# First norm and the projection to queries, keys and values merged into one chunked stage

## The chip, the cores and the metric

The kernel runs on one core of a Trainium2 chip. A core has a matrix engine (TensorE, in the profile PE, with its weight loads as PEld), VectorE (DVE), ScalarE (ACT), GpSimd (POOL), and SyncE, whose queue (SPq) issues transfers. The engines run their own programs in order and meet at semaphores. The metric is the time of one execution in microseconds (us); less is better.

## What is computed

Four steps, each added to its input: an attention with rotary positions and keys and values from a latent of 64, a mixture of experts, a selective state-space layer, and a second mixture of experts. Each has a layer norm ahead of it. The change touches the beginning of the first:

```python
x = L0_attn_x                                   # (4, 1024, 128), float32
xn = (x - m) / sqrt(v + eps)                    # layer norm over the last axis
q = (xn @ wq).reshape(B, T, H, D)               # H = 16, D = 8
lat = xn @ w_down                               # 64 wide
k = (lat @ wk_up).reshape(B, T, H, D)
v = (lat @ wv_up).reshape(B, T, H, D)
q = _apply_rope(q, cos, sin); k = _apply_rope(k, cos, sin)
# scores = q k / sqrt(D), by pages of 32 causal; softmax; attn @ v; @ wo
x = x + attention
```

The rest of the computation is not changed.

## The kernel before

The 4096 tokens lie as 32 tiles of 128 tokens on the partitions (`X`), and as 8 chunks of 512 tokens (`CH`), two to a batch. A stage is a block: every engine runs its part and all meet at a barrier behind it.

The first stage is `norm_transpose` with `load_x=True`. SyncE's queue issues X in four transfers, the two identity matrices, and the eight weights and tables of the projection (line 122). VectorE takes the statistics of all 32 tiles (`tile_stats`, line 85), then forms mean and variance for all 32 at once in seven small operations (lines 147 to 153). GpSimd raises to the power -1/2, four columns at a time (line 132, eight times). VectorE normalises a chunk in four operations (line 162), PE turns it in four transposes through the identity (line 175) into one of two PSUM banks, and ScalarE copies it to `xnT` (line 189). Only then comes the barrier.

The second stage is `project_qkv`. For each chunk PE runs w_down (the latent), wq, wq_swap, and from the stored latent wk, wk_swap and the values (lines 299 to 308). The swapped products are those of the neighbouring column, for the rotation. VectorE rotates: `by_cos`, `by_sin` and their sum `rot` (lines 321, 323, 327; called cos, sin and rotation here). The result is split into three bfloat16 parts: ScalarE stores the first (line 367), GpSimd forms the remainder `rest` (line 351), ScalarE stores the second (line 372), and VectorE, one chunk later, the third (line 334). SyncE's queue writes the parts to DRAM (`write_parts`, six transfers a chunk, line 246), waiting for each part. From chunk 2 on it also issues five row loads a chunk (`load_rows`, line 483), which bring the parts back in the attention's layout: 25 in this stage, the remaining ones in the next. ScalarE waits, before it overwrites a half of `parts`, for the writes two chunks back.

PE's code in this stage is a loop; what holds a matmul is `swap_taken` (VectorE has read the previous chunk's swapped products), `lat_stored` and `v_stored` (ScalarE's copies). The third stage is the attention (`attend`), whose PE program starts when the barrier is passed, the rows of group 0 are loaded and the mask rows are in.

Of the kernel before, what the change touches and what calls it, by code (L numbers as in the profile page):

```python
# [11 lines left out]
ALU = mybir.AluOpType  # L12
# [79 lines left out]
def norm_transpose(nc, g, visit, loads=(), load_x=False):  # L92
# [3 lines left out]
    with ExitStack() as ctx:  # L96
# [10 lines left out]
        if load_x:  # L107
            half_set, stats_ready = sem("half_set"), sem("stats_ready")
        x_loaded = g.second_ring_in
        block = ctx.enter_context(nc.Block())  # L110

        @block.sync
        def _(sp):
            if load_x:
                x_tiles = g.x_dram.rearrange("b (n p) e -> p (b n) e", p=P)
                for b in range(B):
                    sp.dma_start(X[:, b * NT // B:(b + 1) * NT // B, :], x_tiles[:, b * NT // B:(b + 1) * NT // B, :]).then_inc(x_loaded[b], 16)
                for dst, name in ((g.ident, "ident"), (g.identb, "identb")):
                    sp.dma_start(dst[:, :], g.w[name]).then_inc(g.consts_loaded, 16)
            for group in loads:  # L120
                for dst, src in group.pairs:
                    sp.dma_start(dst, src).then_inc(group.loaded, 16)

        @block.gpsimd
        def _(pool):
            if load_x:
                pool.memset(half[:, :], -0.5).then_inc(half_set, 1)
                pool.wait_ge(half_set, 1)
# [6 lines left out]
        def _(dve):  # L135
            dve.sem_inc(transposed, TURNS)
            if load_x:
                for b in range(B):
                    dve.wait_ge(x_loaded[b], 16)
                    for n in range(b * NT // B, (b + 1) * NT // B):  # L140
                        last = tile_stats(dve, g, n)
                last.then_inc(stats_ready, 1)
                dve.wait_ge(stats_ready, 1)
# [106 lines left out]
def project_qkv(nc, g, q):  # L250

    with ExitStack() as ctx:
        sb = lambda name, shape, dt=F32: ctx.enter_context(nc.sbuf_tensor(f"qkv_{name}", shape, dt))
        sem = lambda name: ctx.enter_context(nc.semaphore(f"qkv_{name}"))
        xnT, PS = g.xnT, g.PS
        w_down, wq, wq_swap, wk, wk_swap, wv, cos, sin = q.w_down, q.wq, q.wq_swap, q.wk, q.wk_swap, q.wv, q.cos, q.sin
        latT = sb("latT", [LAT, 2, CH])
        by_cos, by_sin, rest = (sb(n, [P, 2, CH]) for n in ("by_cos", "by_sin", "rest"))
        rot = sb("rot", [P, 2, 2, CH])
        parts, part_ready, written = g.parts, g.part_ready, g.written  # L260
# [3 lines left out]
        block = ctx.enter_context(nc.Block())  # L264

        @block.sync
        def _(sp):
            for k in range(2):
# [9 lines left out]
            for b in range(B):  # L278
                for k in range(CPB):
                    if CPB * b + k < NCH - 1:  # L280
                        write_parts(sp, g, b, k)
                    if CPB * b + k == CPB:
                        for half in range(CPB):
                            sp.wait_ge(written[half], 2 * WRITES)
# [6 lines left out]
        def _(pe):  # L291
            pe.wait_ge(q.loaded, q.all)
# [2073 lines left out]
```

## Time and profile before

| | us |
|---|---|
| median of 3 runs | 1381.78 |
| lowest, highest | 1377.9, 1382.5 |
| profiled execution, its own time | 1377.09 |
| its span | 1375.2 |
| norm stage, until the first projection matmul | 28.8 |
| projection, PE's first to last matmul | 28.8 to 76.3 |
| first matmul of the attention | 87.96 |
| PE busy over the span | 1223.8 (89%) |

The profile is one execution, recorded per instruction. A line of time gives the start and the length of an instruction or of a run of like ones, and in brackets how long its engine was idle before and whose work ended that. Starts are what to compare; a matmul's end is modelled.
### The profile page before, as it was taken

Reading aid. Unit: us, or ns where it says so; the run is one execution under the profiler, and the core shown is the slowest. Engines: PE = TensorE matmul, PEld = TensorE weight load, DVE = VectorE, ACT = ScalarE, POOL = GpSimd, SP = SyncE. Lnnn points to the kernel's source line nnn. Section 1 sums busy time; section 2 is a strip of 40 time slices with the busy share of each in tenths; the row PEclk is TensorE's granted clock in tenths of the full one; section 3 lists DMA queues with packets and bytes.
Section 4 is the critical chain, followed back from the end, with each engine's and each line's share of the span. In section 5 each row is a group of like instructions: output and inputs, shape, how many; then the busy total and the mean of one; then the engine's idle time right before and its main releaser. Section 6 shows DMA issues by size and latency. Waiting matters only on the chain. (4 is left out here: it accounts for less than half of the span.)

```text
span 1375.2 us, 23176 instructions
## 1 busy us (share of the span) xinstructions
PE 1223.8 (89%) x8438; PEld 641.1 (47%) x8438; DVE 1090.1 (79%) x1339; ACT 849.8 (62%) x1505; POOL 573.9 (42%) x424
## 2 busy tenths in 40 slices
PE   4948999999899979899996966999999999975998
PEld 2412343334343435454443334655565556564665
DVE  5779899999899556856554866999999999974554
ACT  2525899899799633232222778989999899602221
POOL 2330000000101138666675024888888889820000
PEclk9966999999999999999996986999999999995999
DMA  4331111321211175333451001322232223111321
GB/s 112 107 125 43 53 54 55 107 64 49 73 48 51 42 104 165 95 104 102 117 97 22 0 6 48 106 91 95 93 98 101 92 92 105 65 29 28 60 61 39
DMA packets 70527, 103.17 MB, mean 75 GB/s; under 512 B 12599, under 2 KB 42247, under 8 KB 70423
## 3 DMA queue, kind: packets, MB, share of 16 engines
q1 hardware_dynamic: 69126, 100.47, 25.7%
q10 hardware_dynamic: 1296, 1.33, 0.3%
q8 instruction: 64, 1.05, 0.3%
q14 instruction: 41, 0.33, 0.1%
HBM read 88.00 MB, written 13.37 MB: 74 GB/s over the span
## 5 line engine op out<-in xcount | busy, mean ns | idle before, releaser
L626 DVE TENSOR_REDUCE att_found<-PS 128x2 f32<-128x1024 f32 (+2 forms) x288 | 332.8, 1219 | 17.7 <-PE PS L735 16.1
L702 ACT ACTIVATE att_prob<-PS 128x512 f32<-128x512 f32 x576 | 313.5, 596 | 44.6 <-PE PS L757 32.8
L1923 POOL TENSOR_TENSOR ms_ch<-xnT,ms_c_rows 128x1024 f32<-128x1024 f32 x103 | 243.8, 2368 | 45.5 <-PE PS L1833 33.4
L1833 PE MATMUL PS<-ms_ch,ident_sb 128*128 128x512 f32 x512 | 241.2, 593 | 1.0 <-POOL ms_ch L1923 1.0
L1884 DVE TENSOR_TENSOR_SCAN xnT<-xnT,PS 128x1024 f32<-128x1024 f32 x103 | 231.1, 2268 | 7.4 <-PE PS L1824 7.1
L1862 ACT ACTIVATE ms_scaled<-m_dtu_turns,m_bt 128x256 f32<-128x256 f32 x448 | 191.6, 495 | 29.5 <-PE PS L1824 29.5
L776 PE MATMUL PS<-att_prob,att_v 128*32 128x256 f32 (+1 forms) x2560 | 184.2, 374 | 2.8 <-ACT fr_out L691 2.6
L1824 PEld LDWEIGHTS PS<-ident_sb,ms_scaled 128*128 128x128 f32 x1024 | 120.6, 144 | 80.1 <-DVE xnT L1884 37.4
L1824 PE MATMUL PS<-ident_sb,ms_scaled 128*128 128x128 f32 x1024 | 137.0, 278 | 9.7 <-ACT ms_scaled L1862 4.6
L735 PE MATMUL PS<-kr,qr 55*128 55x128 bf16 (+4 forms) x1152 | 120.8, 291 | 25.1 <-DVE att_found L626 13.4
L1250 ACT ACTIVATE f_h<-PS,e_w_b 128x512 f32<-128x512 f32 x64 | 43.9, 687 | 137.6 <-PE PS L1401 129.1
L757 PE MATMUL PS<-qr,kr 55*128 55x128 bf16 (+4 forms) x1152 | 115.2, 278 | 13.6 <-ACT att_prob L702 7.5
L1833 PEld LDWEIGHTS PS<-ms_ch,ident_sb 128*128 128x128 f32 x512 | 87.4, 191 | 64.6 <-issue 61.2
L1869 ACT ACTIVATE xnT<-m_dt,m_a 128x1024 f32<-128x1024 f32 x103 | 116.9, 1136 | 0.0
L735 PEld LDWEIGHTS PS<-kr,qr 48*128 48x128 bf16 (+1 forms) x1152 | 39.5, 97 | 133.4 <-issue 94.9
L1231 POOL TENSOR_TENSOR f_yT<-f_yT,f_prod 128x512 f32<-128x512 f32 x56 | 71.1, 1270 | 68.7 <-DVE f_prod L1343 67.5
L1333 DVE SCALAR_TENSOR_TENSOR f_x3s<-PS,e_w_b,f_mask_row 128x512 f32<-128x512 f32 x64 | 48.0, 750 | 61.2 <-PE PS L1405 60.5
L1219 POOL TENSOR_TENSOR f_xm<-xnT,f_gate_row 128x512 f32<-128x512 f32 x64 | 81.3, 1271 | 13.0 <-DMA f_gate_row<-gate_rows_dram 10.7
L776 PEld LDWEIGHTS PS<-att_prob,att_v 128*32 128x32 f32 x2560 | 55.1, 109 | 62.7 <-issue 53.8
L1410 PE MATMUL PS<-f_h,e_w_w 128*128 128x512 f32 x128 | 66.7, 603 | 6.8 <-DVE f_prod L1343 6.7
L2239 ACT ACTIVATE f_sg<-PS 128x512 f32<-128x512 f32 x40 | 23.9, 597 | 78.5 <-PE PS L2222 78.5
L585 POOL TENSOR_TENSOR att_neg<-att_zero,att_row_max 128x32 f32<-128x32 f32 x16 | 4.1, 254 | 162.7 <-DVE att_row_max L639 162.7
(237 smaller groups left out, 1776.6 us busy)
## 6 DMA issues: line engine op xcount, KB each, us to landing
ms_c_rows<-bc_rows_dram SPq DMA_DIRECT2D x64, 512.0 KB, 3.7
f_gate_row<-gate_rows_dram SPq DMA_DIRECT2D x64, 256.0 KB, 3.6
f_mask_row<-mask_rows_dram SPq DMA_DIRECT2D x64, 128.0 KB, 3.2
qk_parts_dram<-parts SPq DMA_DIRECT2D x48, 128.0 KB, 1.9
heads_dram<-fr_out SPq DMA_DIRECT2D x16, 256.0 KB, 2.7
f_mask_row<-mask_rows_dram SPq DMA_DIRECT2D x64, 64.0 KB, 3.3
qr<-qk_parts_dram SPq DMA_DIRECT2D x32, 96.0 KB
qr<-qk_parts_dram SPq DMA_DIRECT2D x96, 32.0 KB
```

The costliest lines, as they stand in the source:

```text
L626: dve.tensor_reduce(found[:, :, pair, first:first + (n - 1) * step + 1:step], PS[:, bank:bank + 2, :].rearrange("p r (w n) -> p r w n", w= ...
L702: act.activation(prob[:, step % PROB_RING * GH + h, :], PS[:, SCORE_BANK + unit % SCORE_RING, :], ACT.Exp, scale=float(D) ** -0.5).then_in ...
L735: last = pe.matmul(PS[:, MAX_BANK + 2 * (m % 2) + r, at:at + n], rows(qr, count, i, pair, r, q_block * P, P), rows(kr, count, i, pair, r, ...
L757: last[r] = pe.matmul(PS[:, SCORE_BANK + (unit + r) % SCORE_RING, col:col + w], rows(kr, count, i, pair, r, j * P, P), rows(qr, count, i, ...
L776: last = pe.matmul(PS[VW * h:VW * (h + 1), VALUE_BANK, q - half * CH:q - half * CH + w], v1[:, i % 2, half, h, j, :], prob[:, step % PROB_ ...
L1219: pool.tensor_tensor(xm[:, e % XM_RING, :], xnT[:, c * CH:(c + 1) * CH], gate_row[:, e % ROW_RING, :], ALU.mult).then_inc(xm_ready, 1)
L1824: last = pe.transpose(PS[:, X_BANK + 2 * half + k // TPC, k % TPC * P:(k % TPC + 1) * P], scaled[:, s % 2, k, half, :], g.ident[:, :])
L1833: last = pe.matmul(PS[:, Y_BANK + 2 * half + q, :], g.ident[:, :], ch[:, half, q * CH:(q + 1) * CH], start=n == 0, stop=n == NS - 1)
L1862: last = act.activation(scaled[:, s % 2, i, :, :], m.dtu_turns[:, TB * b + i, :, :], ACT.Identity, scale=m.bt[:, at:at + 1])
L1869: act.activation(decay_then_h(s, half), m.dt[:, half, sequence(b)], ACT.Exp, scale=m.a[:, half, n:n + 1]).then_inc(decay_ready, 1)
L1884: dve.tensor_tensor_scan(decay_then_h(s, half), decay_then_h(s, half), inputs(half), 0.0, ALU.mult, ALU.add).then_inc(scanned, 1)
L1923: pool.tensor_tensor(ch[:, half, :], decay_then_h(s, half), c_rows[:, s % C_RING, :], ALU.mult).then_inc(ch_ready, 1)
```

## The change

`norm_transpose` no longer serves the first norm; its work moves into `project_qkv`, one block for both. Without the first barrier:

- The eight weights and tables are issued by ScalarE's queue at the start (line 439 of the new file); SyncE's queue issues X, the identities and then the page masks.
- Mean and variance are formed for one batch (8 tiles) at a time: `moments(b)`. `root(b)` on GpSimd takes 8 columns at once. `tmp`, `mean` and `rstd` are small double buffers.
- VectorE normalises chunks 0 and 1, finishes all statistics, and then, in the loop, rotates chunk c, makes the third part of c-1 and normalises c+2; after chunks 1 and 3 it forms the moments of batches 2 and 3.
- PE turns chunks 0 and 1, projects 0, and then for each c turns c+1 and projects c. The turned chunk goes into the latent's bank 6 (chunk 1 into the values' bank 7), so wq comes first and w_down waits for ScalarE's copy of the turned chunk.
- ScalarE copies chunk c+1 (`store`), then the latent of c, then splits c-1.
- All loops are written out instead of running with a register.

The second norm stage is the same code, now counted as the first visit.

```diff
-                norm_transpose(nc, g, 0, [weights], load_x=True)
                 attention(nc, g, weights, f)
...
-                norm_transpose(nc, g, 1, [m, m.last])
+                norm_transpose(nc, g, 0, [m, m.last])
...
         @block.tensor
         def _(pe):
-            pe.wait_ge(q.loaded, q.all)
+            def turn(c):
+                pe.wait_ge(normed, c + 1)
+                if c >= 2:
+                    pe.wait_ge(lat_stored, c - 1)
+                for j in range(TPC):
+                    last = pe.transpose(PS[:, turn_bank(c), j * P:(j + 1) * P], xn[:, c % 2, j, :], ident[:, :])
+                last.then_inc(turned, 1)
+
+            def project(c):
+                k, x = c % 2, xnT[:, c * CH:(c + 1) * CH]
+                pe.wait_ge(x_stored, c + 1)
+                pe.matmul(PS[:, 2 * k, :], wq[:, :], x, start=True, stop=True)
+                if c + 1 < NCH:
+                    pe.wait_ge(x_stored, c + 2)
+                pe.matmul(PS[0:LAT, LAT_BANK, :], w_down[:, :], x, start=True, stop=True).then_inc(lat_done, 1)
+                pe.wait_ge(swap_taken, c + 1)
+                pe.matmul(PS[:, SWAP_BANK, :], wq_swap[:, :], x, start=True, stop=True)
+                pe.wait_ge(lat_stored, c + 1)
+                pe.matmul(PS[:, 2 * k + 1, :], wk[:, :], latT[:, k, :], start=True, stop=True).then_inc(qk_done, 1)
...
+            turn(0)
+            turn(1)
+            pe.wait_ge(q.loaded, q.all)
+            project(0)
+            for c in range(1, NCH):
+                if c + 1 < NCH:
+                    turn(c + 1)
+                project(c)
...
         @block.vector
         def _(dve):
...
+            def normalize(c):
+                b = c // CPB
+                dve.wait_ge(rstd_ready, b + 1)
+                if c >= 2:
+                    dve.wait_ge(turned, c - 1)
...
+            statistics(0)
+            moments(0)
+            statistics(1)
+            normalize(0)
+            normalize(1)
+            moments(1)
+            statistics(2)
+            statistics(3)
+            dve.wait_ge(q.loaded, q.all)
+            for c in range(NCH):
+                rotate(c)
+                if c >= 1:
+                    third(c - 1)
+                if c + 2 < NCH:
+                    normalize(c + 2)
+                if c in (1, 3):
+                    moments(c // 2 + 2)
+            third(NCH - 1)
...
         @block.scalar
         def _(act):
...
+            for dst, src in q.pairs:
+                act.dma_start(dst, src).then_inc(q.loaded, 16)
+            act.preload_act_table(ACT.Copy)
+            store(0)
+            store(1)
+            latent(0)
+            for c in range(1, NCH):
+                if c + 1 < NCH:
+                    store(c + 1)
+                latent(c)
+                split(c - 1)
+            split(NCH - 1)
```

PE, from the program's start on the loop of the projection, before. `norm_xn` and `qkv_xn` are normalised tiles, `qkv_latT` the stored latent; in brackets stand the semaphores that a row waits for.

```order
L302 MATMUL PS<-xnT,qkv_w_wq_swap 128x512 [waits qkv_swap_taken]
L304 MATMUL PS<-qkv_latT,qkv_w_wk 128x512 [waits qkv_lat_stored]
L305 MATMUL PS<-qkv_latT,qkv_w_wk_swap 128x512
L308 MATMUL PS<-qkv_w_wv,qkv_latT 128x128 [waits qkv_v_stored]
L308 MATMUL PS<-qkv_w_wv,qkv_latT 128x128 x3
L299 ISA
L299 MATMUL PS<-xnT,qkv_w_w_down 64x512
L300 MATMUL PS<-xnT,qkv_w_wq 128x512
```

The same engine and place now, from the projection of chunk 0 into that of chunk 1:

```order
L304 MATMUL PS<-xnT,qkv_w_wq_swap 128x512 [waits qkv_swap_taken]
L306 MATMUL PS<-qkv_latT,qkv_w_wk 128x512 [waits qkv_lat_stored]
L307 MATMUL PS<-qkv_latT,qkv_w_wk_swap 128x512
L310 MATMUL PS<-qkv_w_wv,qkv_latT 128x128 [waits qkv_v_stored]
L310 MATMUL PS<-qkv_w_wv,qkv_latT 128x128 x3
L293 MATMUL PS<-ident_sb,qkv_xn 128x128 [waits qkv_lat_stored,qkv_normed]
L293 MATMUL PS<-ident_sb,qkv_xn 128x128 x3
L299 MATMUL PS<-xnT,qkv_w_wq 128x512 [waits qkv_x_stored]
L302 MATMUL PS<-xnT,qkv_w_w_down 64x512 [waits qkv_x_stored]
```

Between the values of a chunk and the first matmul of the next now stand four transposes, and the first of them waits for `qkv_normed`.

VectorE in the projection's loop, before: the rotation of chunk 1, the third part of chunk 0 and the start of chunk 2.

```order
L321 TENSOR_TENSOR qkv_by_cos<-PS,qkv_w_cos 128x1024 [waits qkv_rotated,qkv_qk_done]
L323 TENSOR_TENSOR qkv_by_sin<-PS,qkv_w_sin 128x1024 [waits qkv_swap_done]
L325 REGISTER_ALU [waits qkv_cos_taken]
L327 TENSOR_TENSOR qkv_rot<-qkv_by_cos,qkv_by_sin 128x1024 [waits qkv_rest_ready,qkv_swap_taken]
L333 REGISTER_ALU
L334 TENSOR_TENSOR parts<-qkv_rest,parts 128x1024 [waits part_ready1]
L321 TENSOR_TENSOR qkv_by_cos<-PS,qkv_w_cos 128x1024 [waits qkv_rotated,qkv_qk_done]
```

The same place now:

```order
L363 TENSOR_TENSOR qkv_by_cos<-PS,qkv_w_cos 128x1024 [waits qkv_rotated,qkv_qk_done]
L365 TENSOR_TENSOR qkv_by_sin<-PS,qkv_w_sin 128x1024 [waits qkv_swap_done]
L369 TENSOR_TENSOR qkv_rot<-qkv_by_cos,qkv_by_sin 128x1024 [waits qkv_rest_ready,qkv_swap_taken,qkv_cos_taken]
L374 TENSOR_TENSOR parts<-qkv_rest,parts 128x1024 [waits part_ready1]
L354 TENSOR_SCALAR qkv_xn<-X,qkv_mean,qkv_rstd 128x128 [waits qkv_turned,qkv_rstd_ready]
L354 TENSOR_SCALAR qkv_xn<-X,qkv_mean,qkv_rstd 128x128 x3
```

The normalising of chunk 3 now stands behind the rotation of chunk 1 and the third part of chunk 0.

## Rows read from the trace of the kernel before

**Rows 1.** Stage table: stretch, its length, busy us of each engine, PE clock, DMA share, GB/s.

```profile
core 0: us, PE busy (x) PEld busy (x) DVE busy (x) ACT busy (x) POOL busy (x), PEclk, DMA share, GB/s
28.80:76.30 47.50, 47.48 (x144) 21.08 (x144) 33.61 (x29) 22.92 (x30) 14.89 (x7) 1.00 0.36 110
87.90:124.40 36.50, 22.96 (x151) 6.52 (x151) 34.70 (x33) 7.67 (x14) 7.24 (x14) 0.50 0.17 51
```

**Rows 2.** Lines of time, program start: start us, length us, engine, line, operation [idle before].

```profile
4.63 1.74 SPq L119 DMA_DIRECT2D ident_sb<-ident  x1
...
4.74 1.65 DVE L85 BATCH_NORM_STATS2 stats<-X 128x6 f32<-128x128 f32 x8 [4.74 <-DMA X<-x]
...
13.23 0.18 DVE L153 TENSOR_SCALAR norm_tmp<-norm_tmp 128x32 f32<-128x32 f32 x1
...
16.08 1.11 PE L175 MATMUL PS<-ident_sb,norm_xn 128*128 128x128 f32 x4 [16.08 <-DVE norm_xn L162]
...
17.33 0.60 ACT L189 ACTIVATE xnT<-PS 128x512 f32 x1 [15.31 <-PE PS L175]
```

**Rows 3.** Transfers issued before 12 us (KB, us to landing), and a stage table row.

```profile
ident_sb<-ident SPq DMA_DIRECT2D x1, 64.0 KB, 5.5
...
5.00:10.00 5.00, 0.00 (x0) 0.00 (x0) 4.67 (x24) 0.00 (x0) 0.00 (x0) 1.00 1.21 287
```

**Rows 4.** Lines of time, first projected chunk.

```profile
28.80 1.96 PE L299 MATMUL PS<-xnT,qkv_w_w_down 128*64 x2 [1.80 <-PEq L96]
...
34.61 1.23 DVE L321 TENSOR_TENSOR qkv_by_cos<-PS,qkv_w_cos 128x1024 f32<-128x1024 f32 x1 [8.78 <-PE PS L304]
```

**Rows 5.** Lines of time, PE and VectorE on chunk 2, and eight normalising operations.

```profile
41.91 1.07 PE L299 MATMUL PS<-xnT,qkv_w_w_down 128*64 x2
...
44.82 1.12 PE L304 MATMUL PS<-qkv_latT,qkv_w_wk 64*128 64x512 f32 x2
...
47.62 0.64 PE L299 MATMUL PS<-xnT,qkv_w_w_down 128*64 x1
...
45.98 1.23 DVE L321 TENSOR_TENSOR qkv_by_cos<-PS,qkv_w_cos 128x1024 f32<-128x1024 f32 x1 [0.97 <-PE PS L304]
...
49.51 1.22 DVE L334 TENSOR_TENSOR parts<-qkv_rest,parts 128x1024 bf16<-128x1024 f32 x1
...
18.03 2.34 DVE L162 TENSOR_SCALAR norm_xn<-X,norm_mean,norm_rstd 128x128 f32 x8 [0.47 <-POOL norm_rstd L132]
```

**Rows 6.** Group of the 128x8 root late in the kernel, and four transposes there.

```profile
L2009 POOL TENSOR_TENSOR mo_rstd<-mo_tmp,half 128x8 f32<-128x8 f32 x4 | 6.6, 1640 | 26.7 <-DVE mo_tmp L2034 26.7
...
1227.20 0.60 PE L1971 MATMUL PS<-ident_sb,mo_xn 128*128 128x128 f32 x4
```

**Rows 7.** Lines of time, end of the projection and start of the attention.

```profile
74.57 1.23 DVE L321 TENSOR_TENSOR qkv_by_cos<-PS,qkv_w_cos 128x1024 f32<-128x1024 f32 x1 [0.97 <-PE PS L304]
...
79.78 1.06 ACT L367 ACTIVATE parts<-qkv_rot 128x1024 bf16<-128x1024 f32 x1 [2.81 <-DMA qk_parts_dram<-parts]
...
84.16 1.23 DVE L334 TENSOR_TENSOR parts<-qkv_rest,parts 128x1024 bf16<-128x1024 f32 x1 [4.78 <-ACT parts L372]
...
87.96 1.04 PE L735 MATMUL PS<-kr,qr 48*128 48x384 bf16 x8 [11.68 <-PEq L252]
...
74.22 2.88 SPq L246 DMA_DIRECT2D qk_parts_dram<-parts  x6
...
80.63 2.86 SPq L246 DMA_DIRECT2D qk_parts_dram<-parts  x6
...
83.54 4.88 SPq L483 DMA_DIRECT2D qr<-qk_parts_dram  x6
```

**Rows 8.** Stage table around two short idle spells of PE, columns as in rows 1.

```profile
139.30:141.50 2.20, 0.16 (x6) 0.11 (x4) 1.27 (x2) 0.22 (x1) 0.00 (x0) 1.00 0.12 14
141.50:144.90 3.40, 3.40 (x36) 1.12 (x34) 1.23 (x1) 2.16 (x4) 0.00 (x0) 0.50 0.26 80
...
779.60:781.90 2.30, 0.27 (x1) 0.00 (x1) 2.30 (x5) 2.30 (x7) 0.00 (x0) 1.00 0.00 0
783.20:786.60 3.40, 3.40 (x5) 1.33 (x4) 3.40 (x7) 2.93 (x5) 0.00 (x0) 0.50 0.00 0
```

More of the change, by code:

```diff
@@ L282, in _ @@
                     if CPB * b + k == CPB:
-                        for half in range(CPB):
-                            sp.wait_ge(written[half], 2 * WRITES)
+                        for part in range(CPB):
+                            sp.wait_ge(written[part], 2 * WRITES)
                     for n in range(begun, min(ROWS_BEGUN, begun + ROWS_A_CHUNK) if b > 0 else 0):
@@ L291, in _ @@
         def _(pe):
-            pe.wait_ge(q.loaded, q.all)
+            def turn(c):
[16 more added lines that the diff above has]
+                pe.matmul(PS[:, 2 * k + 1, :], wk[:, :], latT[:, k, :], start=True, stop=True).then_inc(qk_done, 1)
+                pe.matmul(PS[:, SWAP_BANK + 1, :], wk_swap[:, :], latT[:, k, :], start=True, stop=True).then_inc(swap_done, 1)
+                pe.wait_ge(v_stored, c + 1)
+                for j in range(TPC):
+                    last = pe.matmul(PS[:, V_BANK, j * P:(j + 1) * P], latT[:, k, j * P:(j + 1) * P], wv[:, :], start=True, stop=True)
+                last.then_inc(v_done, 1)
@@ L311, in _, with statistics @@
+            turn(1)
[5 more added lines that the diff above has]
+                project(c)
         @block.vector
         def _(dve):
-            dve.sem_inc(rotated, 1)
-            dve.sem_inc(rest_ready, 2)
-            dve.wait_ge(q.loaded, q.all)
-            def rotate(c, k, before):
+            def statistics(b):
+                dve.wait_ge(x_loaded[b], 16)
+                for n in range(b * TB, (b + 1) * TB):
+                    last = tile_stats(dve, g, n)
+                last.then_inc(stats_done, 1)
@@ new lines, in normalize @@
+            def normalize(c):
[3 more added lines that the diff above has]
+                    dve.wait_ge(turned, c - 1)
+                for j in range(TPC):
+                    n = c % CPB * TPC + j
+                    last = dve.tensor_scalar(xn[:, c % 2, j, :], X[:, c * TPC + j, :], mean[:, b % 2, n:n + 1], rstd[:, b % 2, n:n + 1],
+                                             ALU.subtract, ALU.mult)
+                last.then_inc(normed, 1)
@@ L353, in _, with store @@
+            root(0)
+            root(1)
+            for c in range(NCH):
+                if c in (1, 3):
+                    root(c // 2 + 2)
+                pool.wait_ge(part_ready[0], c + 1)
+                pool.wait_ge(part_ready[2], c + 1)
+                pool.tensor_tensor(rest[:, :, :], rot[:, c % 2, :, :], parts[:, c % 2, 0, :, :], ALU.subtract).then_inc(rest_ready, 1)
         @block.scalar
         def _(act):
-            act.preload_act_table(ACT.Copy)
-            def latent(c, k, reused):
+            def store(c):
+                act.wait_ge(turned, c + 1)
+                act.activation(xnT[:, c * CH:(c + 1) * CH], PS[:, turn_bank(c), :], ACT.Copy).then_inc(x_stored, 1)
```

120 lines of the change are left out of this document (50 added, 70 removed).

## The prediction

> **What bounds the kernel now.** I read the stages first, then the lines of time inside the two that the change merges, then what ends them. The stage table [rows 1] gives the projection 47.5 us, from 28.8 to 76.3, in which PE (TensorE) is busy 47.48: PE is the bound there. The norm ahead of it takes the first 28.8 us: all 32 tiles' statistics must be in before the first moment is formed, and the first projection matmul starts when the last chunk is turned [rows 2, 4]. After 76.3 PE is idle for 11.6 us, until the attention's first matmul at 87.96 [rows 7]. What holds it is the tail of this stage: SyncE's queue issues the row loads of chunk 6 from 83.54, five of which belong to this stage (the sixth row load is already the next stage's), to about 87.6, and VectorE ends its last third part at 85.4 [rows 7]. So 87.6 is the time to beat: everything behind it (1287 us) runs the same code from there, and I let it only shift.
>
> In the steady state before, a chunk costs 5.72 us: the rotation's first product, cos, starts at 45.98 for chunk 2 and at 74.57 for chunk 7, 28.59 over five chunks [rows 5, 7]. PE issues its six matmuls of 0.95 us back to back (41.91 to 47.62) and never waits for VectorE, whose four operations a chunk (4.75 us from the start of cos to the end of the third part, 45.98 to 50.73) run beside the next chunk's matmuls [rows 5].
>
> **Part 1, the start.** The first chunk now needs the statistics of 8 tiles, not of 32, and no barrier. On VectorE: X's first quarter lands at 4.74 before, its statistics take 1.65 [rows 2], seven small operations of about 0.2 each, as the last one's 0.18, 1.5, the root on 8 columns 1.64 (the same operation elsewhere in the kernel [rows 6]), and four normalising operations 1.2 (eight took 2.34 [rows 5]). That is 10.8 if nothing else moved. But the transposes need the identity, which stands behind all of X on SyncE's queue and landed at 4.63 + 5.5 = 10.1 [rows 2, 3]. Now 1.3 MB of weights go at the same time on ScalarE's queue. The transfers moved 287 GB/s while busy [rows 3], and all of it together is 3.5 MB (X 2.1, weights 1.3, identities 0.1), 12.2 us. So the identity lands between 10.1 and 13.9; I take 13.5, near the upper end, because the rate shown was already full with X alone. Issue time is saved on SyncE, but nothing waited for it; the eight issues on ScalarE end long before its first copy.
>
> The Trainium skill ("DMA: Bandwidth & Descriptors", Issuing engines are not separate DMA queues) says the same of the queues: all issuers' transfers run on the same 16 engines, so a second queue saves only sequencer time. If the second queue did add rate, the start would be 2.7 us earlier than I take it, and the total with it.
>
> From the first transpose: four transposes at the low rate and the handover 1.25, the copy 0.60, a handover 0.1 [rows 2], so the first projection matmul starts at 15.4. Before, it took 5.81 from the first matmul (28.80) to cos (34.61), the first alone 1.96 [rows 4]; I keep that, since PE comes equally cold. **cos of chunk 0 starts at 21.2 instead of 34.61: 13.4 us gained.** The statistics and moments of the other batches lie on VectorE before that and fit.
>
> **Part 2, the loop.** Here a wait is added. PE's order is: turn chunk c+1, then project chunk c. The turn waits for `normed`, and VectorE normalises c+1 only after rotating c-1 and making the third part of c-2. "Two chunks ahead" holds for VectorE's normalising; PE turns only one ahead, and as its queue is in order the six matmuls of chunk c, whose input has long been stored, stand behind the turn. VectorE's rotation of c in turn waits for PE's fourth matmul of chunk c. So the two take turns. One round, at PE's full rate:
> - VectorE, from the start of cos: 4.75 to the end of the third part, 1.2 to normalise, 0.1 to hand over: 6.05 [rows 5].
> - PE, from the first transpose: four of them, 0.11 apart, 0.44 (four end after 0.60 [rows 6]). w_down also waits for ScalarE's copy: 0.60 + 0.14 + 0.60 + 0.07 = 1.41, the same as 0.44 + 0.95. Then w_down and wq_swap, 1.91, and 1.16 from the start of wk (44.82) to cos (45.98) [rows 5]: 4.5.
> Sum 10.5 us a round against 5.72. Only wk_swap and the value matmuls (1.9 us of PE) lie beside VectorE's part. The third part of c-1 waits for its split, which ScalarE now begins only after the latent copy of chunk c. That copy ends 1.3 before cos (w_down starts 3.07 before cos; 1.07 for it, 0.1, and 0.6 for the copy), and from the split's start to the third part it took 79.78 to 84.16, 4.4 [rows 7]: ready 3.1 after the start of cos, taken at 3.53, so it does not wait, by 0.4. The moments after chunks 1 and 3 lie under PE's part.
>
> The chunks: chunk 0 has no third part before it, so cos of chunk 1 comes 3.53 + 1.2 + 0.1 + 4.5 = 9.3 later, at 30.5. Five rounds of 10.5 follow: cos of chunk 6 at 83.0. There is no turn ahead of chunk 7, so it follows after PE's own 5.7: 88.7. The tail: third part of chunk 6 done at 88.7 + 4.75 = 93.5, its two writes 1.0, five row loads at 0.81 (83.54, 4.88 for six [rows 7]) 4.1: **98.6, against 87.6: 11.0 us later** with PE at full rate. SyncE's issue chain, which paced the end before, now follows. ScalarE's wait for the writes of chunk 5 (79.78 before [rows 7]) goes, and the chain behind chunk 7 (rotation 3.7, then the 4.4 above, then 1.23: 9.4 from cos) ends at 98.1, just covered. The same 11.6 us idle of PE becomes about 8 before the attention; the clock was at 0.50 through that stage's first 36.5 us [rows 1] and I expect that again.
>
> **Part 3, the clock.** In each round PE is idle 10.5 - 6.2 = 4.3 us. The trace has two shorter idle spells after full work: 139.3 to 141.5, after which the granted clock was 0.50 for 3.4 us, and 779.6 to 781.9, after which it was 0.50 from 783.2 to 786.6 [rows 8]. 0.50 is 1.2 GHz of 2.4. If each of the six spells brings one such stretch wholly over PE's part, PE does 1.7 us less work in each. The bounds are 0, if it falls and recovers within the idle time or not at all, and about 4.5 a round, if PE stays low through all of its part, as over the attention's start [rows 1]. I take 1.5, because some of a stretch will lie in idle time: 6 x 1.5 = 9.0.
>
> The Trainium skill ("TensorE: Matmul & The Clock Gate", HAM oscillation) describes this: bursts of matmuls with waits between lose the full clock again and again. By that rule part 3 recurs in every round; the two spells above agree.
>
> **Sum.** +11.0 + 9.0 = +20.0 us. The profiled run took 1377.1 (span 1375.2), so 1397.1. That run lies below the three timed ones (median 1381.8, lowest 1377.9); putting the base between, at about 1379, gives 1399.
>
> **Rivals.**
> - *The clock holds* (the idle spells cost nothing): +11, 1390. Against it stand both spells of rows 8; for it, that PE comes back to a dense run of 6.2 us each time. If the identity also lands early it is +8.5, 1387.
> - *The clock stays low through most rounds*: six times 4.5 and about 4 for chunk 7 on top of +11, +42, 1421. Against it: in both spells of rows 8 the clock came back after 3.4 us of work. Half of it would be 1410.
> - *It gets faster: the turn's wait is covered.* If normalising c+1 were done when PE comes to its turn, a chunk would cost PE 0.44 + 5.72 = 6.2, SyncE's 6.4 (74.22 to 80.63 [rows 7]) would pace the end, and the 13.4 us of part 1 would mostly stay: about -11, 1368. The sign turns at a round of 10.5 - 11.0/6 = 8.7 us without any clock loss. VectorE's own 6.05 would have to overlap with PE's 4.5 by 1.8 more, and no operation of either can start sooner in the order shown. An error in a duration of 0.2 us does not reach it.
> - *The same*, within 0.3% (about 4 us, what a measurement of this kernel can tell from no change): a round of 8.5 to 9.2 us, between the two.
>
> **How the numbers follow.** Forecast 0.58; the clock holds 0.22; low through most rounds 0.12; faster 0.04; the same 0.04. The likeliest gives 1399. The range reaches from the clock holding with an early start (1387, less 1 for the base) to half way to the low-clock case (1410, plus 2 for the base): 1386 to 1412. Slower holds the first three, 0.92.
>
> **What would show it.** cos of chunk 0 between 18.5 and 22; distance of later cos starts 10.5 to 13, not 5.7; PE's transposes waiting for the normalising on VectorE about 4 us, six times; the first matmul of the attention at 99 to 110; granted clock 0.50 in part of nearly every round. A distance near 6.2 would refute part 2; a clock of 1.00 throughout, part 3; an identity before 11, part 1. I would be wrong as a whole if the attention behind the stage did not just shift.

## The result and the profile after

The changed kernel takes 1405.27 us (median of 4 runs, 1402.15 to 1406.8), the kernel before 1380.78 beside it (4 runs, 1377.9 to 1382.5). The ratio is 1.0184, 95% interval 1.0170 to 1.0199: slower by 24.5 us, inside the forecast's range of 1386 to 1412 and 6 above its middle. The profiled execution took 1405.07 us, span 1403.3. It lies at its median, while the profiled execution before (1377.09) was the fastest of its kind, so the two profiles lie further apart (28.1 us in span) than the medians.

Lines of time of the changed kernel at its start (start us, length us, engine, line, operation [idle before <- what ended it]), to hold against [rows 2]:

```profile
5.02 2.32 SPq L263 DMA_DIRECT2D ident_sb<-ident  x1
5.10 1.64 DVE L85 BATCH_NORM_STATS2 stats<-X 128x6 f32<-128x128 f32 x8 [5.10 <-DMA X<-x]
7.38 0.43 SPq L263 DMA_DIRECT2D identb_sb<-identb  x1
7.96 1.64 POOL L401 TENSOR_TENSOR qkv_rstd<-qkv_tmp,half 128x8 f32<-128x8 f32 x1 [7.10 <-DVE qkv_tmp L345]
9.64 2.14 DVE L354 TENSOR_SCALAR qkv_xn<-X,qkv_mean,qkv_rstd 128x128 f32<-128x128 f32 x8 [0.15 <-POOL qkv_rstd L401]
15.43 1.94 PE L293 MATMUL PS<-ident_sb,qkv_xn 128*128 128x128 f32 x8 [15.43 <-DMA identb_sb<-identb]
17.30 1.19 PE L299 MATMUL PS<-xnT,qkv_w_wq 128*128 128x512 f32 x1
```

Both chunks are normalised by 11.8, and PE waits until 15.43 for the identities. The first matmul of the projection is at 17.30 (28.80 before [rows 4]), the first cos product at 22.77.

One whole round, from the cos product of chunk 2 to that of chunk 3, and the handover to PE in it:

```profile
46.90 1.22 DVE L363 TENSOR_TENSOR qkv_by_cos<-PS,qkv_w_cos 128x1024 f32<-128x1024 f32 x1 [5.15 <-PE PS L306]
50.49 1.22 DVE L374 TENSOR_TENSOR parts<-qkv_rest,parts 128x1024 bf16<-128x1024 f32 x1
51.62 1.11 DVE L354 TENSOR_SCALAR qkv_xn<-X,qkv_mean,qkv_rstd 128x128 f32<-128x128 f32 x4
52.78 1.12 PE L293 MATMUL PS<-ident_sb,qkv_xn 128*128 128x128 f32 x4 [4.23 <-DVE qkv_xn L354]
53.69 1.92 PE L299 MATMUL PS<-xnT,qkv_w_wq 128*128 128x512 f32 x2
55.54 1.94 PE L302 MATMUL PS<-xnT,qkv_w_w_down 128*64 128x512 f32 x2
57.40 1.13 PE L304 MATMUL PS<-xnT,qkv_w_wq_swap 128*128 128x512 f32 x2
58.46 1.12 PE L306 MATMUL PS<-qkv_latT,qkv_w_wk 64*128 64x512 f32 x2
59.62 1.23 DVE L363 TENSOR_TENSOR qkv_by_cos<-PS,qkv_w_cos 128x1024 f32<-128x1024 f32 x1 [6.89 <-PE PS L306]
```

VectorE works from 46.90 to 52.73 and then waits 6.89 us. PE waits 4.23, turns, projects at half speed (a matmul, recorded as two instructions, takes 1.9 us until 57.4 and then 1.1), and hands back. Only wk_swap and the values run beside VectorE's part; the rest of the two parts is one after the other. The waits of PE between 22 and 104 us (total, times, longest) show how often:

```profile
PE PS L293 <- DVE qkv_xn L354: 24.1, 6, 4.2
```

The stage table (columns as in [rows 1]): the six rounds with a turn, two stretches inside them, and the first part of the attention:

```profile
22.80:98.00 75.20, 51.12 (x133) 21.68 (x132) 34.95 (x61) 20.96 (x29) 14.36 (x8) 0.77 0.19 63
26.80:33.60 6.80, 6.07 (x10) 2.04 (x10) 0.67 (x3) 1.91 (x3) 0.00 (x0) 0.51 0.00 0
40.60:43.70 3.10, 2.83 (x7) 1.33 (x8) 1.05 (x8) 0.60 (x1) 1.64 (x1) 0.51 0.25 85
114.90:152.00 37.10, 23.66 (x155) 6.62 (x155) 34.60 (x33) 7.85 (x14) 7.13 (x14) 0.50 0.16 51
```

Where the first row of [rows 1] had PE busy all the time at 1.00, PE is now busy 51.1 of 75.2 us at a mean of 0.77. The second row spans one stretch at 0.50 and the third lies inside another, which lasts 3.4 us (40.5 to 43.9). Four of the six rounds have a stretch of 6.8 us, the second and the sixth one of 3.4. The attention's start looks as it did, at 0.50 for its first 37 us. The end of the stage:

```profile
103.95 1.23 DVE L363 TENSOR_TENSOR qkv_by_cos<-PS,qkv_w_cos 128x1024 f32<-128x1024 f32 x1 [1.11 <-PE PS L306]
106.78 3.20 SPq L227 DMA_DIRECT2D qk_parts_dram<-parts  x6
110.02 5.32 SPq L550 DMA_DIRECT2D qr<-qk_parts_dram  x6
112.15 1.23 DVE L374 TENSOR_TENSOR parts<-qkv_rest,parts 128x1024 bf16<-128x1024 f32 x1 [3.39 <-ACT parts L436]
114.87 1.04 PE L802 MATMUL PS<-kr,qr 48*128 48x384 bf16 x8 [9.21 <-PEq L233]
```

The attention starts at 114.87 against 87.96 [rows 7], 26.9 us later, and the profiled executions end 28.1 apart in span. What lies between shifts, but for 1.2 us.

### The profile page after: what moved, and what is told of

Same layout as the page of the kernel before. It is cut to its first block and busy times, and to the rows that moved or that the text cites. A ratio compares the mean times of both kernels' runs of the same rounds, so it can differ in the third digit from the quotient of the medians.

```text
span 1403.3 us, 22962 instructions
## 1 busy us (share of the span) xinstructions
PE 1236.9 (88%) x8438; PEld 642.7 (46%) x8438; DVE 1091.1 (78%) x1360; ACT 847.3 (60%) x1504; POOL 572.1 (41%) x420
## 5 line engine op out<-in xcount | busy, mean ns | idle before, releaser
L1900 PE MATMUL PS<-ms_ch,ident_sb 128*128 128x512 f32 x512 | 241.2, 594 | 0.9 <-POOL ms_ch L1990 0.9
L1317 ACT ACTIVATE f_h<-PS,e_w_b 128x512 f32<-128x512 f32 x64 | 43.9, 687 | 138.1 <-PE PS L1468 127.8
L1900 PEld LDWEIGHTS PS<-ms_ch,ident_sb 128*128 128x128 f32 x512 | 87.4, 191 | 64.5 <-issue 61.2
L1286 POOL TENSOR_TENSOR f_xm<-xnT,f_gate_row 128x512 f32<-128x512 f32 x64 | 81.1, 1268 | 14.3 <-DMA f_gate_row<-gate_rows_dram 12.7
```

The lines of the kernel that those rows point to most:

```text
L1286: pool.tensor_tensor(xm[:, e % XM_RING, :], xnT[:, c * CH:(c + 1) * CH], gate_row[:, e % ROW_RING, :], ALU.mult).then_inc(xm_ready, 1)
L1900: last = pe.matmul(PS[:, Y_BANK + 2 * half + q, :], g.ident[:, :], ch[:, half, q * CH:(q + 1) * CH], start=n == 0, stop=n == NS - 1)
```

## Experiments

Each kernel differs from the changed one as its diff shows, and was timed beside the kernel before. "cos 0" and "cos 7" are the starts of these products and "attention" that of its first matmul, in the profiled execution. The medians of the kernel before, as measured beside them, lie between 1378 and 1381, so the ratio is what to compare. A round is the time from one cos product to the next.

| kernel | cos 0 | cos 7 | attention | median us | ratio [95%] |
|---|---|---|---|---|---|
| before | 34.61 | 74.57 | 87.96 | 1380.8 | 1 |
| changed | 22.77 | 103.95 | 114.87 | 1405.3 | 1.0184 [1.0170, 1.0199] |
| fill_idle | 23.16 | 91.68 | 102.59 | 1391.5 | 1.0079 [1.0058, 1.0100] |
| norm_first | 22.84 | 69.38 | 80.14 | 1371.3 | 0.9941 [0.9916, 0.9965] |
| turn_inside | 23.62 | 74.42 | 85.00 | 1374.9 | 0.9976 [0.9954, 0.9998] |
| root_later | 22.70 | 72.60 | 83.13 | 1373.8 | 0.9965 [0.9949, 0.9981] |
| pool_beside_2 | 22.50 | 109.41 | 121.58 | 1413.0 | 1.0247 [1.0218, 1.0277] |
| ident_first | 20.34 | 101.19 | 111.83 | 1404.4 | 1.0170 [1.0136, 1.0205] |
| weights_sync | 23.20 | 104.58 | 115.11 | 1404.2 | 1.0176 [1.0157, 1.0195] |
| root_later_ident_first | 20.47 | 71.78 | 82.37 | 1371.9 | 0.9952 [0.9934, 0.9969] |
| norm_root_ident | 19.92 | 67.49 | 78.48 | 1367.3 | 0.9927 [0.9909, 0.9945] |
| norm_first_ident_first_2 | 19.15 | 65.70 | 76.39 | 1364.6 | 0.9910 [0.9883, 0.9937] |
| moments_early_2 | 20.54 | 64.25 | 75.44 | 1367.5 | 0.9922 [0.9899, 0.9945] |

### Is it the place of the normalising on VectorE? (norm_first)

```diff
             for c in range(NCH):
+                if c + 2 < NCH:
+                    normalize(c + 2)
                 rotate(c)
                 if c >= 1:
                     third(c - 1)
-                if c + 2 < NCH:
-                    normalize(c + 2)
-                if c in (1, 3):
+                if c in (0, 2):
                     moments(c // 2 + 2)
```

(GpSimd's two later roots move with the moments.)

> The changed kernel with one thing moved: VectorE normalises chunk c+2 ahead of rotating chunk c instead of behind it (and the moments of batches 2 and 3 one chunk earlier, so that the normalising finds them). PE's order stays. Theory (the turn of c+1 waits for VectorE's whole previous round): the wait goes, cos starts come every 6.3 to 6.6 us instead of 12 to 13, PE's clock stays at 1.00 from chunk 0 on, cos of chunk 7 near 68, first matmul of the attention near 79 (before: 87.96, changed kernel: 114.87), time near 1372. Rival (the rounds are long because of what turning inside the loop costs PE and ScalarE, four transposes, their copy and the order of the copies): the rounds stay over 9 us and the time over 1390.

Measured: 1371.3 us, attention at 80.14. The rounds are 6.3, 7.0, 6.8, 7.6, 6.5, 6.5 and 5.9 us. In the stage table PE is busy 38.3 of 40.7 us and the clock never falls:

```profile
22.80:63.50 40.70, 38.27 (x133) 17.36 (x133) 34.34 (x58) 20.42 (x29) 14.38 (x8) 1.00 0.33 108
```

Same work, same pipeline depth, one call in another place: the slow-down of 1.8% becomes a gain of 0.6%. The wait of the turn for `normed` is the cause, both of the serial rounds and of the clock loss in them.

### What of it is clock? (fill_idle)

Four matmuls whose result nobody uses are given to PE ahead of each turn's wait. They do not make the normalising any earlier; they only fill the time until it is done (at most 0.60 us of waiting is left).

```diff
+            def fill(c):
+                pe.wait_ge(lat_stored, c)
+                for _ in range(4):
+                    pe.matmul(PS[:, LAT_BANK, :], wq[:, :], xnT[:, 0:CH], start=True, stop=True)
+
             def turn(c):
+                if c >= 2:
+                    fill(c - 1)
                 pe.wait_ge(normed, c + 1)
```

> The changed kernel plus work: ahead of each wait for the normalised chunk (six times) PE runs four 128x512 float32 matmuls of 0.95 us into the latent's bank, whose result nobody reads. Theory (in each round PE's clock falls in the idle spell of about 4.2 us, and that costs 1.4 to 2.9 us a round): the clock stays at 1.00 from about 21 us to the end of the projection, rounds are 10.5 us, cos of chunk 7 near 91, attention near 102, and the time falls by about 12 to near 1393, although PE does 24 more matmuls. Rival (the rounds are over 10.5 for another reason, such as ScalarE's copies coming late): the rounds stay at 12 to 13, time 1405 or more.

Measured: 1391.5 us, attention at 102.59 (102 expected). The clock is 1.00 through the rounds, which are 9.7, 10.6, 10.55, 10.6, 10.56, 10.55 and 5.9 us:

```profile
23.20:85.80 62.60, 59.76 (x181) 26.03 (x180) 34.98 (x62) 20.97 (x29) 14.43 (x8) 1.00 0.22 74
```

This is the kernel of the rival "the clock holds": 3.7 us of extra matmuls in each round make it 13.8 us faster. From cos 0 to cos 7 it takes 68.5 us against 81.2, so the low clock costs the changed kernel 12.7 us, 2.1 a round, and the serial rounds cost the rest.

### The other way to take the wait out (turn_inside, root_later)

PE's turn of chunk c+1 goes into the projection of chunk c, behind wk_swap, and ScalarE's copy behind that of the values.

```diff
                 if c >= 2:
-                    pe.wait_ge(lat_stored, c - 1)
+                    pe.wait_ge(lat_stored, c)
...
                 pe.matmul(PS[:, SWAP_BANK + 1, :], wk_swap[:, :], latT[:, k, :], start=True, stop=True).then_inc(swap_done, 1)
+                if 1 <= c < NCH - 1:
+                    turn(c + 1)
                 pe.wait_ge(v_stored, c + 1)
```

> The changed kernel with PE's and ScalarE's order changed and VectorE's left: PE turns chunk c+1 inside the projection of chunk c, behind wk_swap and ahead of the values (not ahead of the whole projection), and ScalarE copies it between V and the second part. Theory: the matmuls of chunk c no longer stand behind the turn of c+1, whose normalising ended a round earlier; rounds 6.2 to 6.6 us, clock 1.00, attention near 79, time near 1372, the same as with the normalising moved. Rival (VectorE's load of 6 us a chunk cannot run beside PE's in either order, or the copy's place delays the first matmul of the next chunk): rounds of 7.5 us or more, time over 1380.

Measured: 1374.9 us, attention at 85.00, 6 us later than expected. Two rounds took 8.9 us (from 36.28) and 9.2 us (from 45.16). In the first VectorE is slow for a reason of its own. Lines of time of VectorE and GpSimd in it:

```profile
37.93 2.13 POOL L413 TENSOR_TENSOR qkv_rest<-qkv_rot,parts 128x1024 f32<-128x1024 f32 x1
38.73 2.40 DVE L369 TENSOR_TENSOR qkv_rot<-qkv_by_cos,qkv_by_sin 128x1024 f32<-128x1024 f32 x1
...
42.32 2.92 DVE L354 TENSOR_SCALAR qkv_xn<-X,qkv_mean,qkv_rstd 128x128 f32<-128x128 f32 x4
42.65 2.24 POOL L413 TENSOR_TENSOR qkv_rest<-qkv_rot,parts 128x1024 f32<-128x1024 f32 x1 [2.60 <-ACT parts L431]
```

In the second VectorE is as fast as elsewhere (sum 1.23, normalising 1.11). There PE had waited 1.59 us for the slow normalising, and the clock was 0.50 from 45.1 to 51.9:

```profile
45.29 1.11 PE L293 MATMUL PS<-ident_sb,qkv_xn 128*128 128x128 f32 x4 [1.59 <-DVE qkv_xn L354]
48.33 2.07 PE L299 MATMUL PS<-xnT,qkv_w_wq 128*128 128x512 f32 x2
```

The length of a wait alone does not say whether the clock falls: in norm_first PE waited 1.54 us, until 47.28, for ScalarE's copy, and stayed at 1.00.

In the first of the two rounds the rotation's sum takes 2.40 in place of 1.23 and the four normalising operations 2.92 in place of 1.11, each beside GpSimd's remainder. The remainder at 37.93 was late because the root of the next quarter stood ahead of it, so I moved that root behind it (root_later):

```diff
             for c in range(NCH):
-                if c in (1, 3):
-                    root(c // 2 + 2)
                 pool.wait_ge(part_ready[0], c + 1)
                 pool.wait_ge(part_ready[2], c + 1)
                 pool.tensor_tensor(rest[:, :, :], rot[:, c % 2, :, :], parts[:, c % 2, 0, :, :], ALU.subtract).then_inc(rest_ready, 1)
+                if c in (1, 3):
+                    root(c // 2 + 2)
```

> The kernel that turns inside the projection (turn_inside), with GpSimd's root of batches 2 and 3 behind the remainder of chunks 1 and 3 instead of ahead of it. In turn_inside the remainder of chunk 1 ran from 37.93, behind the root, beside VectorE's rotation, which then took 2.40 us instead of 1.23 and ended 1.07 after GpSimd; the next normalising took 2.92 instead of 1.11. Theory (an operation of VectorE whose operands all lie in SBUF is held while GpSimd works, and the root pushes GpSimd's remainder onto it): all rotations take 1.23, rounds are 6.7 us throughout, the low clock at 45 to 51 us goes, attention near 79.5 instead of 85.0, time near 1370. Rival (VectorE's long operations come from a late semaphore elsewhere): the rotation of chunk 2 still takes over 2 us.

Measured: 1373.8 us, attention at 83.13; 79.5 was expected. The sum is back at 1.23, but the next collisions took its place: normalising at 41.96 is again 2.94 us, and a small operation of the moments, 0.17 elsewhere, took 2.04:

```profile
34.77 2.12 POOL L411 TENSOR_TENSOR qkv_rest<-qkv_rot,parts 128x1024 f32<-128x1024 f32 x1 [4.57 <-ACT parts L431]
34.88 2.04 DVE L343 SCALAR_TENSOR_TENSOR qkv_tmp<-qkv_tmp 128x8 f32<-128x8 f32 x1
```

An operation on 128x8 numbers that takes 2 us is not slowed by its own work. Three rounds are long, 8.7, 7.6 and 7.7 us; in the third VectorE is not slow, and PE runs at 0.50 for 3.4 us of it, after a wait of 2.18 us for the normalising.

### VectorE beside GpSimd, measured by itself (pool_beside_2)

The changed kernel, with one more operation on GpSimd over a tensor that nobody else touches. It starts when the third part is made, which is when VectorE begins to normalise. In the rounds that normalise it ends long before the remainder can start; in the last two chunks it stands right ahead of it.

```diff
             for c in range(NCH):
...
-                pool.wait_ge(part_ready[0], c + 1)
                 pool.wait_ge(part_ready[2], c + 1)
+                if c >= 1:
+                    pool.wait_ge(half_set, 1 + c)
+                    pool.tensor_tensor(idle[:, :, :], idle[:, :, :], idle[:, :, :], ALU.subtract).then_inc(half_set, 1)
+                pool.wait_ge(part_ready[0], c + 1)
```

> The changed kernel with one more operation of GpSimd per chunk: a 128x1024 subtraction of a tensor of its own by itself, put ahead of the remainder, so that it starts when the third part of the chunk before is made, which is when VectorE begins to normalise. It uses nothing that VectorE reads or writes, and ends some 4 us before the remainder may start. Theory (an operation of VectorE that reads SBUF alone is held while GpSimd runs over SBUF): normalising four tiles takes 2.9 us in place of 1.11 in the six rounds, the rounds grow by 1.8 each, first attention matmul 114.9 + 11 = 126, total 1416. Rival (the 2.9 us of the earlier kernels came from the data that both work on, or from something else of their order): normalising stays at 1.11, total 1405.

Measured: 1413.0 us, attention at 121.58. I had overlooked that in two rounds the root (1.64 us) stands in front of the new operation, and in the first there is none yet. That makes a better test than the one meant, since the same kernel has both cases. Normalising, and the new operation where it fell beside:

```profile
39.15 1.11 DVE L355 TENSOR_SCALAR qkv_xn<-X,qkv_mean,qkv_rstd 128x128 f32<-128x128 f32 x4
42.87 1.89 POOL L416 TENSOR_TENSOR qkv_idle<-qkv_idle 128x1024 f32<-128x1024 f32 x1
...
52.56 2.69 DVE L355 TENSOR_SCALAR qkv_xn<-X,qkv_mean,qkv_rstd 128x128 f32<-128x128 f32 x4
52.72 1.93 POOL L416 TENSOR_TENSOR qkv_idle<-qkv_idle 128x1024 f32<-128x1024 f32 x1 [3.91 <-DVE parts L375]
```

Three times the two overlap and normalising takes 2.69 us; three times they don't and it takes 1.11. The data have nothing in common, so the cause lies in what the two engines share; that this is the access to SBUF fits all the traces here but is not shown by itself. The rival falls. Three times 1.6 us is 4.7 of the 6.7 at the attention; PE's waits grow by the same (5.8 us at 55.30). Another 1.3 arise behind the last cos product (12.2 us to the attention for 10.9), where the new operation stands right ahead of the last remainder. What is left, under 1 us, goes with the clock: all six rounds now have a stretch of 6.8 us at 0.50, where the changed kernel had four, and the mean over the rounds is 0.75 in place of 0.77. The 11 us expected were six collisions, of which three came.

### The start (ident_first, weights_sync)

The identities are issued ahead of X:

```diff
+            for dst, name in ((g.ident, "ident"), (g.identb, "identb")):
+                sp.dma_start(dst[:, :], g.w[name]).then_inc(g.consts_loaded, 16)
             x_tiles = g.x_dram.rearrange("b (n p) e -> p (b n) e", p=P)
...
-            for dst, name in ((g.ident, "ident"), (g.identb, "identb")):
-                sp.dma_start(dst[:, :], g.w[name]).then_inc(g.consts_loaded, 16)
```

> The changed kernel with the two identity matrices issued ahead of X on SyncE's queue. Theory (the first transposes wait for the identities, which landed at 15.4 because they stand behind X while the weights share the transfer engines): the first transpose starts near 11.1, with VectorE's first normalised chunk; the first projection matmul then waits for the weights, near 13.4 instead of 17.3; cos of chunk 0 near 19.3 instead of 22.8, time near 1401.5. Rival (the start is bound by the sum of all bytes, which does not change): the first projection matmul still near 17, time 1405.

Measured: the transposes start at 12.40 in place of 15.43, now held by the normalising, cos 0 is at 20.34 (19.3 expected) and the attention at 111.83, 3.0 us earlier. X now stands behind the identities, and its statistics start at 6.70 instead of 5.10, which is why the transposes were not there at 11.1 as expected. The total of 1404.4 can't be told from 1405.3. The second kernel leaves X and the identities as in the changed one and moves the eight weight loads from ScalarE's queue to SyncE's, behind the identities:

```diff
+            for dst, src in q.pairs:
+                sp.dma_start(dst, src).then_inc(q.loaded, 16)
             for k in range(2):
...
-            for dst, src in q.pairs:
-                act.dma_start(dst, src).then_inc(q.loaded, 16)
```

> The changed kernel with the weights and tables issued by SyncE's queue behind the identities, as before, and nothing by ScalarE's. Theory (all transfers share the engines, and what is issued beside X only delays what is behind X): the identities land near 10.1 instead of 15.4, the first transpose starts near 11, the weights are in at 15.1, the first projection matmul starts near 15.3 instead of 17.3, the attention 2 us earlier than in the changed kernel (near 113), time near 1403. Rival (a second queue brings the weights in sooner and that is what the start needs): the first projection matmul later than 17.3.

Measured: PE has both identities at 11.13, 4.3 us earlier, and the attention starts at 115.11 (113 expected). The second identity is issued 0.8 us earlier and then takes 4.2 us to land, not 7.8. What ran beside them is what delayed them. In this kernel the four page loads, too, were issued only behind the weights, at 11.65 instead of 8.0, so the run does not part the weights (1.3 MB) from those loads (0.35 MB); at 287 GB/s [rows 3] the loads are 1.2 us by themselves, an estimate.

```profile
6.62 0.43 SPq L263 DMA_DIRECT2D identb_sb<-identb  x1
11.13 1.94 PE L295 MATMUL PS<-ident_sb,qkv_xn 128*128 128x128 f32 x8 [11.13 <-DMA identb_sb<-identb]
16.21 2.08 PE L301 MATMUL PS<-xnT,qkv_w_wq 128*128 128x512 f32 x2 [3.14 <-DMA qkv_w_sin<-sin]
```
 The weights now come last and PE waits for them until 16.21. That is 1.1 earlier than in the changed kernel, but the first three matmuls take 2.0 us each, where there only the first did, and cos 0 is at 23.20. Which queue carries the weights is worth nothing here.

### Putting it together

Three kernels combine what was found: root_later with the identities first, norm_first with the identities first and the later roots behind the remainder, and norm_first with the identities first alone.

> root_later with the identities ahead of X. If the two gains add: attention near 76.5, time near 1367.5. If the shorter start is eaten by SyncE's queue (its writes and row loads of 6.4 to 6.5 us a chunk already as long as a round of PE): attention no earlier than in root_later.

> norm_first (VectorE normalises ahead of the rotation) with the identities ahead of X and GpSimd's root behind the remainder. norm_first had the attention at 80.14 and one round of 7.6 us, beside a root. Theory: that round shrinks to 6.6, the start is 3 us earlier, attention near 76.5, time near 1367. Rival (the long round is a wait of the normalising for its root, which now comes later still): that round grows, attention at 79 or later.

> Normalising ahead of the rotation and the identities ahead of X, with the later roots ahead of the remainder on GpSimd's queue. It differs from norm_first by the identities alone, and from norm_root_ident by the place of two roots alone. Theory (each term adds on its own): cosine product of chunk 0 at 19.9 to 20.5, first attention matmul 77.5, total 1369, that is 2.5 under norm_first. Rival (the identities gave nothing at the end, the roots did): attention at 80, total 1371.

The identities gave 0.8 us at the attention on root_later (82.37, where 76.5 was expected) and 3.75 on norm_first (76.39, where 77.5 was expected). By the ratios the total is 0.3% lower, some 4 us, with overlapping intervals. On root_later the start was 2.2 us earlier, but 1.4 of it went in one round of 9.2 for 7.7 us. Moving the roots did not help: 78.48 with it, 76.39 without, of which 0.8 are there at cos 0. In the kernel with the roots behind, normalising collides with the remainder twice, 2.94 and 2.95 us, and the rounds there are 8.6 and 7.6 us. The root was ready each time, so the rival (a wait for the root) falls too. So the last kernel makes all moments and roots before the first rotation, in time that VectorE had idle. The mean and the root are kept for four quarters instead of two.

```diff
             statistics(2)
+            moments(2)
             statistics(3)
+            moments(3)
...
-                if c in (0, 2):
-                    moments(c // 2 + 2)
```

> The kernel with normalising ahead of the rotation, identities first, and now all moments and roots ahead of the first rotation (mean and root are kept for all four quarters), so that no small operation of VectorE and no normalising falls beside GpSimd's remainder any more. Theory (the two rounds of 7.6 and 8.6 us come from what VectorE has beside GpSimd, not from the clock): all seven rounds 5.9 to 6.5, cosine products from 20 to 65, first attention matmul 76.0 against 78.5, total 1364.5 against 1367. Rival (the long rounds come of something else): rounds of 7 to 8.6 remain, total 1367.

All rounds but the first (5.1) and the last (5.9) are 6.5 to 6.75 us, and normalising fits in the 1.3 us ahead of the remainder:

```profile
37.15 1.11 DVE L354 TENSOR_SCALAR qkv_xn<-X,qkv_mean,qkv_rstd 128x128 f32<-128x128 f32 x4
38.41 2.12 POOL L413 TENSOR_TENSOR qkv_rest<-qkv_rot,parts 128x1024 f32<-128x1024 f32 x1 [4.35 <-ACT parts L431]
...
75.44 1.04 PE L802 MATMUL PS<-kr,qr 48*128 48x384 bf16 x8 [9.48 <-PEq L233]
```

The attention starts 12.5 us earlier than in the kernel before, 0.5 better than expected. In the total it is not better than norm_first_ident_first: 1367.5 against 1364.6, with overlapping intervals. The profiled executions differ where both run the same code: from L1770 to L1900 it is 113.3 us (743.2 to 856.5) against 107.4 (738.1 to 845.5), and between 700 and 900 us their mean clock is 0.80 against 0.85. These are the slowest execution of the one kernel (1374.7) and the fastest of the other (1363.7). I can't say what sets that; a gain of 1 us at the attention is lost in it. Both kernels beat the kernel before, by 0.8 to 0.9%.

## Why the prediction held, and where its terms were off

The total fell into the range, and slower was right, but no error covered another: all terms erred to the same side, and three of the forecast's own signs failed. cos 0 came at 22.77 (18.5 to 22 was named), two rounds took 13.2 and 13.4 us (10.5 to 13), and the attention started at 114.87 (99 to 110). That the total still lay inside is owed to the width of the range, which went 13 us above the likeliest value.

At the attention the forecast was +20.0 us and the trace has +26.9. Split at the first and the last cos product:

| | forecast | measured |
|---|---|---|
| start, to cos 0 | -13.4 | -11.8 (22.77 for 34.61) |
| cos 0 to cos 7, full clock | +27.5 | +28.5 (fill_idle, 68.5 for 40.0) |
| clock in the rounds | +9.0 | +12.7 (81.2 less 68.5) |
| cos 7 to the end of the stage | -3.1 | -2.5 (10.9 for 13.4) |
| sum | +20.0 | +26.9 |

**Part 1, the start: right in kind, 1.6 us too good.** The wait was for the identities, as said, but PE waits for both, and I had taken the first. That one landed at 14.3 (issued at 5.02, 9.3 us to landing), already above my upper end of 13.9. The second is issued at 7.38, after the first one's issue had taken 2.32 us, and was ready at 15.4. The upper end counted X, the weights and the identities, but SyncE issues four page loads of 0.35 MB in all from 8.0 on. With them 3.85 MB at 287 GB/s end near 15.1, counted from 1.7 as in the 13.9; that is an estimate, which would fit, but no run leaves those loads out alone. weights_sync shows the other side: with weights and page loads behind them both are there at 11.1. cos followed 5.5 us after the first projection matmul, 5.8 forecast.

**Part 2, the loop: right.** Six serial rounds with a wait of 4.2 us each (3.1 in the first), and the one with no turn at 5.9. At full clock a round is 10.55 us against 10.5, which fill_idle showed; that the order of the calls makes it so, norm_first and turn_inside showed by two different edits. The third part never waits except the last one, as forecast. The clause "no operation of either can start sooner in the order shown" was the whole point, since one call further up undoes it.

**Part 3, the clock: the right one of three cases, its size too small.** The six rounds took 2.9, 1.4, 2.2, 2.7, 2.9 and 1.4 us more than the forecast's full-clock rounds. The term was 1.5 each; by fill_idle it is 2.1. The step that failed is the 1.7 us, read from one stretch of 3.4 us at 0.50 [rows 8]: the trace after has two stretches of 3.4 us (as 40.5 to 43.9) and four of 6.8 us (as 26.8 to 33.6). A low stretch of 6.8 us covers the turn and three matmuls, and the round with it loses nearly 3 us. The rounds that cost 1.4 are the ones with a short stretch. Both rivals of the clock fall, "holds" by 12.7 us and "low throughout" by the rounds at 1.00 in their second halves. The Trainium skill ("TensorE: Matmul & The Clock Gate", HAM oscillation) describes the mechanism, a wait after which the next burst of matmuls starts at the low clock, round after round. The trace agrees: each of the six waits, of 3.1 to 4.2 us, was followed by a turn at 0.50.

**The tail** came 0.6 us longer. The row loads begin 6.1 us after cos 7 (5.75 forecast), and the six took 5.32 us to issue for 4.88 [rows 7], so that five cost 0.4 more. Behind it everything shifted, as forecast: of the 28.1 us between the spans, 26.9 are there at the attention's first matmul.

At the attention the forecast was thus 6.9 us low, made of +1.6, +1.0, +3.7 and +0.6 us. In the profiled executions 1.2 us more arise behind it (1405.1 against 1397.1). The medians differ by 6.3 (1405.3 against 1399), because the base of 1379 had already allowed 1.9 us for the fast profile of the kernel before.

## What to carry to other kernels

When a stage runs ahead of another on a shared in-order engine, count "ahead" at each engine: here the normalising was two chunks ahead on VectorE, but its place behind the rotation left PE's turn no lead at all, and moving one call before the rotation turned a loss of 1.8% into a gain of 0.6%, and of 0.9% with the identities loaded first. A short wait in every round of a matmul loop can cost more than itself, because the matmuls after it may run at the low clock; what it costs can be measured by filling the wait with matmuls that nobody needs. Before adding an operation to VectorE, look at what GpSimd runs beside it.

## What the runs showed of the hardware

- **GpSimd can hold VectorE up where VectorE's tensors all lie in SBUF, whatever the size of its operation.** Beside a 128x1024 subtraction on GpSimd (2.1 us) four normalising operations took 2.69 to 2.95 us for 1.11, a 128x1024 sum 2.40 for 1.23, and one 128x8 operation 2.04 for 0.17. Each ends 0.03 to 1.1 us behind GpSimd's. The products that read PSUM (cos at 46.90 beside a remainder from 46.35) kept their 1.22. The Trainium skill ("SBUF — State Buffer", SBUF: two separate sides) has the rule: the two engines share a port pair, which one of them locks for a whole instruction, against operations of VectorE in a two-port mode or with two SBUF inputs. The traces agree where GpSimd subtracts, and do not where it forms the root, which also reads SBUF: in norm_first normalising at 41.88 took 1.12 while the 128x8 root ran on GpSimd from 41.92 for 1.64, and in the kernel before eight normalising operations at 18.03 took 2.34 beside the roots [rows 5] and as long at 23.50 with GpSimd idle. So the length of GpSimd's instruction does not decide it; what does, the operation or how much it reads, no run here parts. Lines of the kernel before:

```profile
13.56 7.94 POOL L132 TENSOR_TENSOR norm_rstd<-norm_tmp,half 128x4 f32<-128x4 f32 x8 [12.71 <-DVE norm_tmp L153]
23.50 2.33 DVE L162 TENSOR_SCALAR norm_xn<-X,norm_mean,norm_rstd 128x128 f32 x8 [0.40 <-PE PS L175]
```

- **A filled wait is cheaper than an empty one.** 3.7 us of useless matmuls in each of six waits of about 4.2 us saved 12.7 us up to the last cos product and 1.0% of the kernel's time.
- **What a second DMA queue carries delayed the first.** With 1.3 MB of weights on ScalarE's queue, and 0.35 MB of page loads right behind the identities on SyncE's, the identities arrived at 15.4 us; with both behind them, at 11.1. They were issued on SyncE's queue in both kernels, the second 0.8 us later in the first case.
